# Expert results of seven slots turned by transposing DMA transfers instead of TensorE transposes

## What is computed

```
x = hidden_states.reshape(-1, H)                      # 2048 x 256
probs = softmax(x @ gate_w.T); w, idx = top_k(probs, 2); w = w / sum(w)
for each expert e (gup: 2048 x 256, dn: 256 x 1024):
    g, u = split(x @ gup.T, 2)
    acc = acc + combine[:, e] * (silu(g) * u @ dn.T)
```

## Time and profile before

| what | value |
|---|---|
| median of 3 runs | 555.14 us (554.34 to 555.21) |
| the profiled execution, its own time | 548.71 us |
| its span, first to last instruction | 547.0 us |
| mean granted TensorE clock over the span | 0.963 |
| expert stage in the trace, first `up` to the end of the span | 257.4 to 547.0 us |
| passes 7 to 13, in which the change acts | 379.1 to 508.2 us |

### The profile page before, as it was taken

How to read it: one execution, slowest core, us unless ns; L and a number is a source line. 1 busy time by engine, 2 the same in 40 slices (tenths; PEclk the granted TensorE clock), 3 DMA queues, 4 the chain that set the end, 5 groups by cost and what they waited for, 6 DMA issues and landing times.

```text
span 547.0 us, 12125 instructions
## 1 busy us (share of the span) xinstructions
PE 493.4 (90%) x3741; PEld 364.2 (67%) x3756; DVE 385.6 (70%) x797; ACT 343.0 (63%) x650; POOL 278.7 (51%) x356
## 2 busy tenths in 40 slices
PE   4795799999998988798998999999999999999991
PEld 3564466776665655345667987878888888777651
DVE  5770668998877857885877988876777667666551
ACT  2243678988888885574766776765656556545530
POOL 5442646556446453105226665666557555654244
PEclk9998799999999999799999999999999999999995
DMA  8558576876776534563657777866555457654224
GB/s 265 172 180 258 179 199 183 268 209 181 245 216 167 182 99 146 183 185 85 188 103 125 148 170 165 188 104 154 85 105 90 84 89 90 105 67 70 30 30 48
DMA packets 87882, 79.89 MB, mean 146 GB/s; under 512 B 48456, under 2 KB 73832, under 8 KB 87688
## 3 DMA queue, kind: packets, MB, share of 16 engines
q1 hardware_dynamic: 74300, 62.69, 41.5%
q0 software_dynamic: 11856, 16.16, 18.4%
q10 hardware_dynamic: 1668, 0.27, 0.3%
HBM read 49.08 MB, written 22.41 MB: 131 GB/s over the span
## 4 chain that ended last, share of the span: by engine, by line
PE 62%; DVE 10%; DMA 8%; ACT 6%; issue 5%; SPq 5%; POOL 1%; another core or an unknown queue 1%; ACTq 0%; DVEq 0%
PE bank L1551 26%; PE bank L1568 13%; PE bank L1349 4%; PE bank L1335 4%; SPq L489 3%; PE bank L1300 2%; PE bank L1580 2%; DMA q_parts<-WE 2%; PE bank L1372 2%; PE bank L1316 2%; PE bank L1358 2%; DVE FB L1223 2%; DVE FB L1227 2%; DMA WE<-x 2%; ACT FB L926 1%
## 5 line engine op out<-in xcount | busy, mean ns | idle before, releaser
L1551 PE MATMUL bank<-FB,WE 128*128 128x0 bf16 x1440 | 189.1, 282 | 1.1 <-DVE FB L1218 0.7
L1551 PEld LDWEIGHTS bank<-FB,WE 128*128 x1440 | 137.8, 98 | 33.2 <-issue 2.7
L728 POOL DMA_INDIRECT out<-FB,slot_tok x60 | 100.0, 1667 | 90.5 <-DVE FB L1244 84.5
L926 ACT ACTIVATE FB<-FB 128x512 bf16<-128x512 f32 x120 | 75.6, 630 | 70.2 <-DVE FB L1223 63.8
L1227 DVE TENSOR_TENSOR FB<-FB 128x512 bf16<-128x512 f32 x120 | 83.3, 694 | 47.2 <-ACT FB L926 41.9
L1568 PE MATMUL bank<-FB,WE 128*128 128x0 bf16 x720 | 103.8, 280 | 4.2 <-DVE FB L1227 2.1
L1223 DVE TENSOR_TENSOR FB<-FB,bank 128x512 f32<-128x512 f32 x120 | 81.9, 683 | 28.5 <-ACT FB L920 19.0
L719 POOL DMA_INDIRECT FB<-x_parts,slot_tok x60 | 61.7, 1028 | 69.4 <-DMA FB<-FB 27.9
L920 ACT ACTIVATE FB<-bank 128x512 f32<-128x512 f32 x120 | 70.6, 589 | 34.3 <-PE bank L1551 29.0
L1568 PEld LDWEIGHTS bank<-FB,WE 128*128 x720 | 67.7, 98 | 23.4 <-issue 7.7
L645 POOL TENSOR_TENSOR WE<-FB,WE 128x256 bf16<-128x256 f32 x104 | 67.8, 679 | 24.7 <-ACT WE L759 24.7
(11 more groups left out here) (186 smaller groups left out, 624.0 us busy)
## 6 DMA issues: line engine op xcount, KB each, us to landing
FB<-w SPq DMA_DIRECT2D x26, 512.0 KB, 5.2
WE<-w SPq DMA_DIRECT2D x44, 256.0 KB
WE<-q_parts SPq DMA_DIRECT2D x32, 200.0 KB
WE<-x SPq DMA_DIRECT2D x16, 256.0 KB, 5.7
q_parts<-FB SPq DMA_DIRECT2D x32, 128.0 KB
x_parts<-WE SPq DMA_DIRECT2D x20, 128.0 KB, 4.0
out<-WE SPq DMA_DIRECT2D x20, 128.0 KB, 5.1
q_parts<-WE SPq DMA_DIRECT2D x16, 128.0 KB
```

Source lines behind the costliest of these rows:

```text
L728: pool.indirect_dma_start(out=out, out_offset=bass.IndirectOffsetOnAxis(ap=slot_tok[:, c:c + 1].bitcast(U32), axis=0), in_=result_tile(c), ...
L926: nc.scalar.activation(hT[k % 3][:, 0, :], hid[k % 2], ACT.Copy).then_inc(hi_ready, 1)
L1551: ins = nc.tensor.matmul(to, wf[:, bass.ds(at + o, P)], xgT[s % 2][:, 2 * part + kc, :].shape_from_register(long[s % 2]), start=(z == 0), ...
```

## The change

For slots 6 to 12 (`BY_DMA`) the eight TensorE transposes go. In their place, in pass s = 7 to 13 for slot s-1:

1. ScalarE writes the high bf16 part of the result straight from PSUM in chunks 1 and 2 (`result_hi`, in the place of the copy), and VectorE the low part in chunks 2 and 3 (`result_lo`, new).
2. SyncE turns the four tiles, both parts at once, each with a transposing DMA of 128x512 bf16 into `y_sb` (`turn_result`). They stand in its queue in pairs behind the pairs of `turn_tile`.
3. ScalarE multiplies the turned high part of a tile by the routing weight into a half of `turn_bank` (`weighted_hi`, new, chunks 5, 6, 7 and 0 of the next pass). VectorE multiplies the low part by the weight and adds that (`result`, now one `scalar_tensor_tensor`; chunks 6, 7, and 0 and 1 of the next pass).
4. `weighted_hi` of tile c waits for the transposing DMA of its tile and for `y_ready` to count c, that is, for the result of tile c-1.
5. From slot 6 on `hT` has two places instead of three; its third holds two more tiles of `y_sb`.

```diff
+BY_DMA = range(6, NS - 2)
...
+        y_parts = yT.rearrange("p k n -> p (k n)").bitcast(BF16).rearrange("p (i k f) -> p i k f", i=SUB, k=2 * KC)
...
+        def h_buffer(k):
+            return k % 3 if k < FC * BY_DMA[0] else k % 2
...
+        def y_parts_free(engine, s):
+            if s - 1 in BY_DMA:
+                for i in range(SUB):
+                    engine.wait_ge(y_turned[i], 16 * (BY_DMA.index(s - 1) + 1))
...
+            def turn_result(s, i):
+                c = SUB * s + i
+                for kc in range(KC):
+                    sp.wait_ge(yT_ready[kc], s + 1)
+                result_tile_free(sp, c)
+                sp.dma_start(y_sb[i].bitcast(BF16).rearrange("p (k f) -> p k f", k=2 * KC), y_parts[:, i], transpose=True).then_inc(y_turned[i], 16)
...
                     for i in range(2):
                         turn_tile(s + 1, 2 * half + i)
+                    if s - 1 in BY_DMA:
+                        for i in range(2):
+                            turn_result(s - 1, 2 * half + i)
...
+            def result_hi(s, kc):
+                act.wait_ge(d_mm, FC * (s + 1))
+                y_parts_free(act, s)
+                nc.scalar.activation(y_parts[:, :, kc, :], y_bank(s, kc).rearrange("p (i f) -> p i f", i=SUB), ACT.Copy).then_inc(yh_ready, 1)
+
+            def weighted_hi(c):
+                act.wait_ge(y_turned[c % SUB], 16 * (BY_DMA.index(c // SUB) + 1))
+                act.wait_ge(y_ready, c)
+                nc.scalar.activation(turn_bank[:, c % 2 * D:(c % 2 + 1) * D], y_sb[c % SUB].bitcast(BF16)[:, 0:D], ACT.Copy,
+                                     scale=slot_w[:, c:c + 1]).then_inc(yw_ready, 1)
...
                     silu(k)
                     if c in (1, 2) and s > 0:
+                        if s - 1 in BY_DMA:
+                            result_hi(s - 1, c - 1)
...
+                    if c in (5, 6, 7) and s - 1 in BY_DMA:
+                        weighted_hi(SUB * (s - 1) + c - 5)
+                    if c == 0 and s - 2 in BY_DMA:
+                        weighted_hi(SUB * (s - 1) - 1)
...
+            def result_lo(s, kc):
+                dve.wait_ge(yh_ready, KC * BY_DMA.index(s) + kc + 1)
+                nc.vector.tensor_tensor(y_parts[:, :, KC + kc, :], y_bank(s, kc).rearrange("p (i f) -> p i f", i=SUB), y_parts[:, :, kc, :], ALU.subtract).then_inc(yT_ready[kc], 1)
...
+                if c // SUB in BY_DMA:
+                    dve.wait_ge(yw_ready, c - SUB * BY_DMA[0] + 1)
+                    nc.vector.scalar_tensor_tensor(out=y_sb[c % SUB], in0=y_sb[c % SUB].bitcast(BF16)[:, D:2 * D], scalar=slot_w[:, c:c + 1],
+                                                   in1=turn_bank[:, c % 2 * D:(c % 2 + 1) * D], op0=ALU.mult, op1=ALU.add).then_inc(y_ready, 1)
+                    return
...
                     hidden(k)
+                    if s - 1 in BY_DMA:
+                        if c in (2, 3):
+                            result_lo(s - 1, c - 2)
+                        if c in (6, 7):
+                            result(SUB * (s - 1) + c - 6)
...
+                    if s - 2 in BY_DMA:
+                        if c < 2:
+                            result(SUB * (s - 2) + 2 + c)
...
-                    if c == 3 and s > 0:
+                    if c == 3 and s > 0 and s - 1 not in BY_DMA:
                         turned_result(s - 1, 0)
```

More of the change, by code:

```diff
@@ L193, in moe_attention_kernel @@
         yT = ffb(KC * CAP).rearrange("p (k n) -> p k n", k=KC)
-        y_sb = [ffb(D) for _ in range(2)]
+        y_parts = yT.rearrange("p k n -> p (k n)").bitcast(BF16).rearrange("p (i k f) -> p i k f", i=SUB, k=2 * KC)
+        y_sb = [ffb(D) for _ in range(2)] + [hT[2].rearrange("p s n -> p (s n)")[:, 2 * D * i:2 * D * (i + 1)].bitcast(F32) for i in range(2)]
         spare = carver(FB[:, 7680:13312], 5632)
@@ L315, in moe_attention_kernel @@
         y_ready = sem("y_ready")
+        yh_ready = sem("yh_ready")
+        y_turned = [sem(f"y_turned{i}") for i in range(SUB)]
+        yw_ready = sem("yw_ready")
         dve_step = sem("dve_step")
@@ L330, in moe_attention_kernel @@
         late_lo = sem("late_lo")
-        y_out = [sem(f"y_out{p}") for p in range(2)]
+        y_out = [sem(f"y_out{i}") for i in range(SUB)]
         xg_in = [sem(f"xg_in{p}") for p in range(2)]
@@ L439, in result_tile, with result_tile_free, h_before, turned_by_pe @@
         def result_tile(c):
-            return xg[c % 2].bitcast(F32) if LAST <= c < LAST + 2 else y_sb[c % 2]
+            return xg[c % 2].bitcast(F32) if LAST <= c < LAST + 2 else y_sb[c % (SUB if c >= SUB * BY_DMA[0] else 2)]
+        def result_tile_free(engine, c):
+            before = c - (SUB if c >= SUB * BY_DMA[0] + 2 else 2)
+            if before >= 0:
+                engine.wait_ge(y_out[before % SUB], 16 * (before // SUB + 1))
+        def h_buffer(k):
+            return k % 3 if k < FC * BY_DMA[0] else k % 2
+        def h_before(k):
+            return next((j for j in range(k - 1, -1, -1) if h_buffer(j) == h_buffer(k)), None)
+        def turned_by_pe(s):
+            return 2 * (s - sum(n < s for n in BY_DMA))
+        def y_parts_free(engine, s):
+            if s - 1 in BY_DMA:
+                for i in range(SUB):
+                    engine.wait_ge(y_turned[i], 16 * (BY_DMA.index(s - 1) + 1))
+            elif s > 0:
+                engine.wait_ge(yt_mm, turned_by_pe(s))
         @block.sync
@@ L725, in scatter @@
                 if c >= SUB and c % SUB == 0:
[L726 to L727 removed]
+                    for i in range(SUB):
+                        pool.wait_ge(y_out[i], 16 * (c // SUB))
                 pool.indirect_dma_start(out=out, out_offset=bass.IndirectOffsetOnAxis(ap=slot_tok[:, c:c + 1].bitcast(U32), axis=0),
[L729 removed]
+                                        in_=result_tile(c), in_offset=None, compute_op=ALU.add).then_inc(y_out[c % SUB], 16)
             for c in range(SUB + 2):
@@ L747, in _ @@
                 scatter(SUB * (NS - 1) + i)
-            for p in range(2):
-                pool.wait_ge(y_out[p], 8 * NTP)
+            for i in range(SUB):
+                pool.wait_ge(y_out[i], 16 * NS)
         @block.scalar
@@ L1567, in down @@
                         last = c == FC - 1 and wpart == 1
-                        ins = nc.tensor.matmul(to, wf[:, bass.ds(at + o, P)], hT[k % 3][:, part, :].shape_from_register(long[s % 2]),
+                        ins = nc.tensor.matmul(to, wf[:, bass.ds(at + o, P)], hT[h_buffer(k)][:, part, :].shape_from_register(long[s % 2]),
                                                start=first, stop=last, skip_group_check=True)
@@ L1600, in _ @@
                         down(s - 1, FC - 2 + c, at[s - 1])
-                    if c == 3 and s > 0:
+                    if c == 3 and s > 0 and s - 1 not in BY_DMA:
                         turned_result(s - 1, 0)
-                    if c == (6 if s < NS - 1 else 5) and s > 0:
+                    if c == (6 if s < NS - 1 else 5) and s > 0 and s - 1 not in BY_DMA:
                         turned_result(s - 1, 1)
```

29 lines of the change are left out of this document (13 added, 16 removed).

## The result

| | before | changed kernel |
|---|---|---|
| median of the runs in this comparison | 555.17 us | 580.79 us |
| ratio, 95% interval | | 1.049 (1.043 to 1.056) |
| profiled execution | 548.71 us | 575.64 us |
| span | 547.0 us | 573.9 us |
| first `up` of pass 0 starts at | 257.4 us | 259.6 us |

A forecast was written before the change was run, and what follows sets the result against it. TensorE was taken as the bound, with the VectorE-ScalarE loop close behind. Removed transposes against loop openings gave -0.4 us, landings +2.1: +1.7 on 555.14, so 556.8 us, range 553.6 to 561.2.

The forecast's parts named there:

- What bounds the kernel: TensorE, full in passes 9 and 12, with the VectorE-ScalarE loop close behind; removing transposes could gain at most 6.2 us.
- The ring's turn: Low part, product, cast, low part on VectorE and ScalarE: 1.99 us a chunk, 15.9 us a pass, no overlap possible.
- `result_lo`, twice a pass ... fills the hole exactly: nothing: VectorE's new low part, 0.69 us, fits its wait for the cast: no cost, or 0.1 us a pass.
- The bullet on two places of `hT`: The cast of chunk k waits for down(k-2), which ends before SiLU and product do: no cost.
- The openings of the ring: Product, result, weighted copy, cast in series, three times a pass: 0.73 us each, 2.2 us a pass.
- the high bound: Upper end for one opening of the VectorE-ScalarE loop: 0.80 us, with result and copy a few hundredths longer.
- one new wait: ScalarE's `weighted_hi` of tile c waits for VectorE's result of tile c-1, delaying that chunk's cast by 0.73 us.
- Do they land?: Turned tile 0 takes 3.4 us where 2.98 are allowed: 0.42 us in each of passes 7 to 11, +2.1 us.
- the estimate of 2.3 us: Time of a 128 KB transfer by the skill page: 2.0 us fixed plus the bytes at 436 GB/s.
- late landings: Rival: tile 0 takes 4.2 us or more, passes stand 1.2 us at chunk 5's copy; 560.7 us, chance 0.18.
- Faster: Rival: an opening of the VectorE-ScalarE loop costs only 0.47 us; 550.8 us with landings in time, chance 0.12.
- The clock: TensorE's clock below full was listed as a sign that the forecast is wrong; no size given.

The follow-up runs named there:

- f1_two_slots: e6_order with only slots 11 and 12 turned by DMA: 550.82 us against 552.30 for the kernel before, ratio 1.000; passes 7 to 13 take 127.35 us.
- e1_lo_early: The changed kernel with the low part in chunks 1 and 2 instead of 2 and 3: 559.81 us, ratio 1.013 to the kernel before.
- e4_two_buffers: The kernel before with hT in two places instead of three from slot 6 on: 554.98 us against 554.39, ratio 1.003.
- e7_no_reorder: e6_order without the new order in SyncE's queue: 561.90 us, ratio 1.011 to the kernel before; passes 7 to 13 take 130.7 us.
- e6_order: Changed kernel, low part in chunks 1 and 2, tiles 0 to 2 weighted into SBUF, their turns ahead of the second next-slot pair: 561.26 us, ratio 1.002.
- e3_best: Changed kernel, low part a chunk earlier, weighted parts into SBUF, weighted copies in chunks 4 to 7, results in 5, 6, 7, 0: 558.06 us, ratio 1.007.
- e5_late_copy: The kernel before with ScalarE's result copies in chunks 2 and 3 instead of 1 and 2 in passes 7 to 13: 569.16 us, ratio 1.015.
- e2_sbuf: The changed kernel with the weighted high part put into y_parts in SBUF instead of turn_bank, low part left in chunks 2 and 3: 574.77 us, ratio 1.032.
- e6_again: e6_order profiled once more, unchanged: 127.2 us in passes 7 to 13, 134.8 at first.
- e7_again: e7_no_reorder profiled once more, unchanged: 129.3 us in passes 7 to 13, 130.7 at first.

## Why the prediction was wrong

- **What bounds the kernel**: held. The ring's turn is 1.99 to 2.00 us in the changed kernel where nothing opens it, and passes with room got shorter by the 0.87 us of two groups of transposes (f1_two_slots: 19.31 us in pass 12 instead of 20.18).
- **The step that failed** is the bullet "`result_lo`, twice a pass ... fills the hole exactly: nothing". It priced the operation by the hole in VectorE's own timeline and never asked who waits for the semaphore that it counts up. The edit takes `yT_ready[0]` from ScalarE in chunk 1 and gives it to VectorE in chunk 2. Its readers are three: SyncE's turn, which the prediction followed, the TensorE transposes, which are gone, and TensorE's down(s, 0), which reads it for the bank. The runs show 20.1 us in its place (changed against e1_lo_early), the clock included. The four passes 8 to 11, forecast at 73.7 us, took 89.75, and pass 13, forecast 0.9 us shorter, was 3.3 longer.
- **The bullet on two places of `hT`**: right, as it stood (e4_two_buffers); in the changed kernel the cast did wait, but for the stop.
- **The openings of the ring**: the right mechanism, three in a full pass, 0.84 us each instead of 0.73 and above the 0.80 of the high bound: the copy takes 0.476 us where I took 0.41, and the hand-over ahead of it 0.10 where I took 0.04. With the low part in time they cost an estimated 4.5 to 5.9 us (e1_lo_early against the two runs of e7_no_reorder). Having found one new wait, I took it for the whole.
- **"Do they land?"**: +2.1 us forecast, one wait of 0.4 us measured. The median of 2.5 us, and not 3.4, is what the transfers take in the changed kernel. Part of the reason may be the loss itself, as stretched passes leave every transfer more time; no run separates this. In the faster kernels e6_order and e7_no_reorder the median is 3.1 and 3.2, over the 14 and 7 transfers whose landing is in the trace, and the longest 6.9. The page "DMA: Bandwidth & Descriptors" of the Trainium skill gives the figures behind the estimate of 2.3 us, under "Anatomy of one DMA", for the path of GpSimd; these transfers are SyncE's. The 2.5 of the changed kernel are close to it all the same, the 3.1 and 3.2 are not.
- **The rivals**: "late landings" named a long stop of the ring and a time near 561 us. It is what the mended kernels suffer from (18.6 us of waits in e3_best), and mostly at tiles 2 and 3, where the rival had tile 0; not this one. "Faster" never had a chance with two operations of 0.48 us in the opening. The true cause was none of the three, and "an engine waits for a bank" was not looked for.
- **The clock** was named only as something that would make the forecast wrong. It is a term: some 7 us behind five stops.

## What to carry to other kernels

When an operation takes over a semaphore from another, list all the places that wait for it, also those that need the buffer and not the value, and compare where each of the two stands in its engine's order; a move of one chunk behind an engine's main work can cost more than all that the change removes. A hole in an engine's timeline prices that engine's time alone. Transposing DMAs are cheap in engine time, but four more of them in each pass fill one in-order queue with transfers that wait for gathers, and what they release should stand well behind the issue: in the traces here they landed after 2.4 to 5.0 us, and two of them after 6.3 and 6.9.

## What the runs showed of the hardware

- TensorE's clock fell toward its lower level (windows at 0.50 to 0.71) behind the stops in chunk 2 of passes 8, 10, 11, 12 and 13. It did not in pass 9 (1.00), whose chunk 2 was about as long as that of pass 8 (5.65 and 5.76 us, the idle times in it 0.50 and 2.65 us against 0.55 and 2.65), nor in e5_late_copy with stops for the bank of 0.9 to 1.7 us. The length of the stop alone doesn't decide: in e2_sbuf stops of 3.3, 3.1 and 3.4 us in passes 7 to 9 left it at 1.00, and behind one of 2.6 us in pass 11 it was 0.57. Which difference decides, the runs don't tell.
- ScalarE's weighted copy of 128x256 elements, bf16 in and fp32 out with a scale per row, takes 0.476 us into PSUM and 0.50 into SBUF; the nearest rows, without such a scale, were 0.38 and 0.41.
- A transposing DMA of 128x512 bf16 within SBUF lands 2.4 us after its issue at the least; with gathers and two other turns beside it, it took up to 6.9, and a gather 6.4 (2.8 in the median of e6_again and 2.9 in that of e7_again).
